# A feed-forward, attention, feed-forward layer: the setup rewritten, and each feed-forward's first tokens prepared in the block ahead of it

## What is computed

```python
def _L0_ffn_ref(x, ...):
    x = _layernorm(x, norm_g, norm_b)
    se = _layernorm(slot_embeds, slot_g, slot_b) * scale
    logits = jnp.einsum('bnd,esd->bnes', x, se)
    dispatch = jax.nn.softmax(logits, axis=1)
    combine = jax.nn.softmax(logits.reshape(x.shape[0], x.shape[1], -1), axis=-1)
    slots = jnp.einsum('bnd,bnes->besd', x, dispatch)
    gate = jax.nn.gelu(jnp.einsum('besd,edf->besf', slots, Wg) + bg[None, :, None, :], approximate=False)
    up = jnp.einsum('besd,edf->besf', slots, Wu) + bu[None, :, None, :]
    eout = jnp.einsum('besf,efo->beso', gate * up, Wd) + bd[None, :, None, :]
    return jnp.einsum('bns,bso->bno', combine, eout.reshape(eout.shape[0], -1, eout.shape[-1]))
x = x + 0.5 * _L0_ffn_ref(_layernorm(x, axis=-1), ...)
x = x + _L0_attn_ref(_layernorm(x, axis=-1), ...)
x = x + 0.5 * _L0_ffn_ref(_layernorm(x, axis=-1), ...)
```

## Time and profile before

| | us |
|---|---|
| median of three runs | 1928.64 |
| profiled execution, whole | 1929.45 |
| its span, first to last instruction | 1927.7 |
| TensorE busy | 1809.2 |
| VectorE busy | 1319.5 |
| ScalarE busy | 1157.5 |
| GpSimd busy | 819.9 |

### The profile page before, as it was taken

One profiled execution on the slowest core, in us unless ns is written; L12 is line 12 of the kernel. 1 busy time (PEld: TensorE's weight loads), 2 busy tenths in 40 slices (PEclk: granted clock), 3 DMA queues, 4 the chain that ended last, 5 costly groups with the idle time before them and its releaser, 6 DMA issues. The chain is left out here.

```text
span 1927.7 us, 35483 instructions
## 1 busy us (share of the span) xinstructions
PE 1809.2 (94%) x11720; PEld 1621.2 (84%) x11720; DVE 1319.5 (68%) x2369; ACT 1157.5 (60%) x2277; POOL 819.9 (43%) x1029
## 2 busy tenths in 40 slices
PE   1999999999999999949999969999999999999998
PEld 1778888888999999949999957888888789999998
DVE  5866666664799888835555457666665558998886
ACT  1676667666565777624444428666666656567775
POOL 1332424224688755412222214234242357885553
PEclk9999999999999999979999989999999999999999
DMA  2553334323465677621121136324342516556774
GB/s 67 207 186 131 121 145 160 131 86 124 153 224 179 244 257 262 225 82 56 65 65 65 44 124 247 133 103 165 146 153 77 186 55 225 180 185 246 262 263 160
DMA packets 106668, 298.25 MB, mean 155 GB/s; under 512 B 16256, under 2 KB 56320, under 8 KB 94272
## 3 DMA queue, kind: packets, MB, share of 16 engines
q1 hardware_dynamic: 106560, 296.88, 43.2%
HBM read 187.63 MB, written 109.22 MB: 154 GB/s over the span
## 5 line engine op out<-in xcount | busy, mean ns | idle before, releaser
L115 POOL TENSOR_TENSOR pool_carrier<-minus_half 128x1 f32<-128x1 f32 x224 | 63.3, 283 | 657.0 <-PE f2bank L839 199.0
L680 ACT ACTIVATE f1r_lt<-f1bank,slot_shift 128x512 f32<-128x512 f32 x128 | 88.2, 689 | 124.0 <-PE f1bank L810 123.9
L680 ACT ACTIVATE f2r_lt<-f2bank,slot_shift 128x512 f32<-128x512 f32 x128 | 88.2, 689 | 123.4 <-PE f2bank L810 123.3
L535 DVE TENSOR_TENSOR f2r_e_lo<-f2bank,f2r_e_hi 128x512 fp32r<-128x512 f32 x128 | 82.4, 684 | 96.3 <-ACT f2r_e_hi L762 96.3
L535 DVE TENSOR_TENSOR f1r_e_lo<-f1bank,f1r_e_hi 128x512 fp32r<-128x512 f32 x128 | 82.4, 684 | 96.3 <-ACT f1r_e_hi L762 96.3
L1498 PE MATMUL f2bank<-f2c_eo,f2c_e_hi 128*128 128x258 f32 (+1 forms) x512 | 129.9, 286 | 0.5 <-DVE f2c_xout L1420 0.5
L1498 PE MATMUL f1bank<-f1c_eo,f1c_e_hi 128*128 128x258 f32 (+1 forms) x512 | 129.9, 286 | 0.5 <-DVE f1c_xout L1420 0.4
L1499 PE MATMUL f1bank<-f1c_eo,f1c_e_hi 128*128 128x256 f32 (+1 forms) x512 | 128.0, 282 | 0.0
L1499 PE MATMUL f2bank<-f2c_eo,f2c_e_hi 128*128 128x256 f32 (+1 forms) x512 | 128.0, 282 | 0.0
L1369 POOL TENSOR_TENSOR f2c_e_lo<-f2c_lt,f2c_e_hi 128x512 fp32r<-128x512 f32 x64 | 82.8, 1295 | 74.8 <-ACT f2c_e_hi L1472 74.8
L1369 POOL TENSOR_TENSOR f1c_e_lo<-f1c_lt,f1c_e_hi 128x512 fp32r<-128x512 f32 x64 | 82.8, 1295 | 74.8 <-ACT f1c_e_hi L1472 74.8
(11 more groups left out here) (321 smaller groups left out, 6624.5 us busy)
## 6 DMA issues: line engine op xcount, KB each, us to landing
logits<-f1r_lt SPq DMA_DIRECT2D x16, 2048.0 KB, 7.3
f1c_lt<-logits SPq DMA_DIRECT2D x32, 1024.0 KB, 7.2
logits<-f2r_lt SPq DMA_DIRECT2D x16, 2048.0 KB, 7.3
f2c_lt<-logits SPq DMA_DIRECT2D x32, 1024.0 KB, 7.0
f1r_xin<-in_L_attn_x SPq DMA_DIRECT2D x16, 512.0 KB, 4.6
normalized<-f1r_xin SPq DMA_DIRECT2D x16, 512.0 KB, 2.7
f1r_xback<-normalized SPq DMA_DIRECT2D x16, 512.0 KB, 8.0
f1e_raw_g<-in_L_ffn_Wg SPq DMA_DIRECT2D x16, 512.0 KB, 4.0
```

The lines of the kernel that those rows point to most:

```text
L115: pool.tensor_tensor(c["pool_carrier"][:, col:col + 1], c["minus_half"][:, 0:1], c["minus_half"][:, 0:1], ALU.add)
L535: dve.tensor_tensor(e_lo[t % 2][:, h * BANK:(h + 1) * BANK], ps_t[h][:, :], rd(e_hi[t % 2][:, h * BANK:(h + 1) * BANK]), ALU.subtract).the ...
L680: act.activation(lt[:, g, sc, :], ps_l[sc % 2][:, :], ACT.Identity, bias=c["slot_shift"][:, sc:sc + 1]).then_inc(logit_out, 1)
```

## The change

It has three parts.

1. `setup_stage`. The slot embeddings are loaded in four DMAs with a semaphore each; then the tokens of group 0, `scale`, four loads of `norm_g`, `slot_g`, `slot_b` and `norm_b` as columns (256 single elements each), three rows, the tokens of group 1 and the biases. DVE only normalizes. PE transposes the normalized embeddings, each of four units into a bank of its own, and ACT applies gain and offset per partition (`gains`, `offsets`, which POOL makes) while it reads PSUM, then makes the high part from the result. The low parts are made by DVE (units 0, 1) and POOL (2, 3). The shift is made from products on POOL and sums on DVE.
2. `first_tokens` prepares group 0 of a feed-forward in the block ahead of it: loads of groups 0 and 1, and for group 0 statistics, scale, normalization, transposes, high and low part. For f1 this is in the setup, for f2 in attention's last turns. The route no longer does this for group 0, and raises the semaphores by hand. In group 0, four units of matmuls stand ahead of the transposes of group 1, where it was one. `token_places` gives both blocks the same places in SBUF; attention's raw weights are freed after its weights block.
3. Attention's last stores are not waited for at the end of its block. The route of f2 waits for them (`x_stored`), on SP, behind the store of the first normalized tokens.

```diff
+def first_tokens(al, c, tag, tk, x_in, banks):
...
+    def load(sp, i):
+        sp.dma_start(tk.xin[i][:, :, :], x_g[i]).then_inc(loaded[i], DMA)
...
+    def scale(pool):
+        pool_wait(pool, c, mv_done, GT)
+        pool.tensor_scalar(tk.var_eps[0][:, :], tk.mv[0][:, :, 1], 1.0 + EPS, EPS * EPS, ALU.mult, ALU.add).then_inc(var_done, 1)
...
+    def hi(act):
+        for k in range(KD):
+            act.wait_ge(tr_done, k + 1)
+            act.activation(tk.xT_hi[0][:, k, :], banks[k][:, :], ACT.Copy).then_inc(hi_done, 1)
+
+    def lo(dve, k):
+        dve.wait_ge(hi_done, k + 1)
+        dve.tensor_tensor(tk.xT_lo[0][:, k, :], banks[k][:, :], rd(tk.xT_hi[0][:, k, :]), ALU.subtract).then_inc(lo_done, 1)
...
+        def embeds_lo(eng, n):
+            h, k = units[n]
+            half = slice(h * BANK, (h + 1) * BANK)
+            eng.wait_ge(hi_done, n + 1)
+            return eng.tensor_tensor(c["emb_lo"][:, k, half], weights[:, k, half], rd(c["emb_hi"][:, k, half]), ALU.subtract)
...
+            slots = prm["slot_embeds"].rearrange("e s d -> (e s) d").rearrange("(t p) d -> p t d", p=P)
+            for i in range(4):
+                sp.dma_start(emb[:, i * PER:(i + 1) * PER, :], slots[:, i * PER:(i + 1) * PER, :]).then_inc(emb_loaded[i], DMA)
+            tokens.load(sp, 0)
+            sp.dma_start(scale[:, :], row(prm["scale"])).then_inc(columns_loaded, DMA)
+            for place, v in ((c["gain"][:, :], "norm_g"), (columns[:, 0, :], "slot_g"), (columns[:, 1, :], "slot_b"),
+                             (c["shift"][:, :], "norm_b")):
+                sp.dma_start(place.unsqueeze(2), prm[v].rearrange("(k p a) -> p k a", p=P, a=1),
+                             allow_slow_non_contiguous=True).then_inc(columns_loaded, DMA)
+            for place, v in ((slot_g, "slot_g"), (norm_b, "norm_b"), (slot_b, "slot_b")):
+                sp.dma_start(place[:, :], row(prm[v])).then_inc(rows_loaded, DMA)
+            tokens.load(sp, 1)
             for i, name in enumerate(("bg", "bu")):
-                sp.dma_start(bias_rows[:, i, :], prm[name].rearrange("e (c p) -> (e c) p", p=P)).then_inc(loads, DMA)
-            sp.wait_ge(loads, LOADS * DMA)
+                sp.dma_start(bias_rows[:, i, :], prm[name].rearrange("e (c p) -> (e c) p", p=P)).then_inc(bias_loaded, DMA)
...
+            pool.wait_ge(columns_loaded, 5 * DMA)
+            pool.tensor_scalar(scaled_gain[:, :], c["gain"][:, :], scale[:, 0:1], 0.0, ALU.mult, ALU.add).then_inc(gain_step, 1)
+            pool.wait_ge(gain_step, 1)
+            pool.tensor_tensor(gains[:, :], scaled_gain[:, :], columns[:, 0, :], ALU.mult).then_inc(gain_step, 1)
+            pool.tensor_tensor(offsets[:, :], scaled_gain[:, :], columns[:, 1, :], ALU.mult).then_inc(gain_step, 1)
+            tokens.scale(pool)
+
+            pool.wait_ge(rows_loaded, 3 * DMA)
+            pool.tensor_tensor(both_g[:, :], slot_g[:, :], norm_b[:, :], ALU.mult).then_inc(row_step, 1)
+            pool.tensor_tensor(both_b[:, :], slot_b[:, :], norm_b[:, :], ALU.mult).then_inc(row_step, 1)
+            for h in range(HB):
+                half = slice(h * NSC // HB, (h + 1) * NSC // HB)
+                pool.wait_ge(row_step, 1)
+                pool.wait_ge(emb_done, (h + 1) * NSC // HB)
+                pool.tensor_tensor(product[:, half, :], emb[:, half, :], both_g[:, :].unsqueeze(1).to_broadcast([P, NSC // HB, D]),
+                                   ALU.mult).then_inc(product_done, 1)
+            for n in range(KD, KD * HB):
+                embeds_lo(pool, n).then_inc(lo_by_pool, 1)
...
+            def shift_sums(h):
+                half = slice(h * NSC // HB, (h + 1) * NSC // HB)
+                dve.wait_ge(product_done, h + 1)
+                dve.tensor_reduce(shift_sum[:, half], product[:, half, :], AX_X, ALU.add).then_inc(sum_done, 1)
...
+            tokens.statistics(dve)
             dve.wait_ge(rstd_done, 1)
             dve.wait_ge(mv_done, NSC)
             for t in range(NSC):
                 dve.tensor_scalar(emb[:, t, :], emb[:, t, :], mv[:, t, 0:1], rstd[:, t:t + 1],
-                                  ALU.subtract, ALU.mult).then_inc(emb_step, 1)
-            dve.wait_ge(emb_step, NSC)
-            dve.tensor_tensor(emb[:, :, :], emb[:, :, :], slot_g[:, :].unsqueeze(1).to_broadcast([P, NSC, D]),
-                              ALU.mult).then_inc(emb_step, 1)
-            dve.wait_ge(emb_step, NSC + 1)
-            dve.tensor_tensor(emb[:, :, :], emb[:, :, :], slot_b[:, :].unsqueeze(1).to_broadcast([P, NSC, D]),
-                              ALU.add).then_inc(emb_step, 1)
-            dve.wait_ge(emb_step, NSC + 2)
-            dve.tensor_scalar(emb[:, :, :], emb[:, :, :], scale[:, 0:1], None, ALU.mult).then_inc(emb_step, 1)
-
-            dve.wait_ge(emb_step, NSC + 3)
-            dve.tensor_tensor(shifted[:, :, :], emb[:, :, :], norm_b[:, :].unsqueeze(1).to_broadcast([P, NSC, D]),
-                              ALU.mult).then_inc(emb_step, 1)
-            dve.tensor_tensor(emb[:, :, :], emb[:, :, :], norm_g[:, :].unsqueeze(1).to_broadcast([P, NSC, D]),
-                              ALU.mult).then_inc(emb_done, 1)
-            dve.wait_ge(emb_step, NSC + 4)
-            dve.tensor_reduce(c["slot_shift"][:, :], shifted[:, :, :], AX_X, ALU.add).then_inc(emb_step, 1)
-
-            for n in range(KD * HB):
-                k, h = n // HB, n % HB
-                dve.wait_ge(hi_done, n + 1)
-                dve.tensor_tensor(c["emb_lo"][:, k, h * BANK:(h + 1) * BANK], tr[n % 2][:, :],
-                                  rd(c["emb_hi"][:, k, h * BANK:(h + 1) * BANK]), ALU.subtract).then_inc(lo_done, 1)
+                                  ALU.subtract, ALU.mult).then_inc(emb_done, 1)
+            tokens.normalize(dve)
+            for n in range(KD):
+                embeds_lo(dve, n).then_inc(lo_by_dve, 1)
+            dve.wait_ge(row_step, 2)
+            dve.tensor_reduce(shift_all[:, :], both_b[:, :], AX_X, ALU.add).then_inc(sum_done, 1)
+            for h in range(HB):
+                shift_sums(h)
+            for k in range(KD):
+                tokens.lo(dve, k)
+            dve.wait_ge(sum_done, 1 + HB)
+            dve.tensor_scalar(c["slot_shift"][:, :], shift_sum[:, :], shift_all[:, 0:1], scale[:, 0:1],
+                              ALU.add, ALU.mult).then_inc(shift_done, 1)
...
+            pe.wait_ge(gain_step, 3)
+            for n, (h, k) in enumerate(units):
+                pe.wait_ge(emb_done, (h + 1) * NSC // HB)
                 for j in range(BANK // P):
...
+            for n, (h, k) in enumerate(units):
+                half = slice(h * BANK, (h + 1) * BANK)
                 act.wait_ge(tr_done, n + 1)
-                act.activation(c["emb_hi"][:, k, h * BANK:(h + 1) * BANK], tr[n % 2][:, :], ACT.Copy).then_inc(hi_done, 1)
+                act.activation(weights[:, k, half], tr[n][:, :], ACT.Identity, bias=offsets[:, k:k + 1],
+                               scale=gains[:, k:k + 1]).then_inc(weights_done, 1)
+                act.wait_ge(weights_done, n + 1)
+                act.activation(c["emb_hi"][:, k, half], weights[:, k, half], ACT.Copy).then_inc(hi_done, 1)
+            tokens.hi(act)
...
-        load_x(0, 0)
-        load_x(1, 1)
         store_xn(0, 0, 0, 0)
+        for s, value in x_stored:
+            sp.wait_ge(s, value)
         sp.wait_ge(xT_tr, KD)
         sp.wait_ge(xn_stored[0], DMA)
         load_x(2, 0)
...
-        norm_scale(0, 0)
+        for s in (xs_done, var_done, rstd_done):
+            pool.sem_inc(s, 1)
         norm_scale(1, 1)
 
...
-        token_stats(0, 0)
         token_stats(1, 1)
-        normalize(0)
         normalize(1)
-        for k in range(KD):
-            transposed_lo(0, 0, k)
...
-        for k in range(KD):
-            transposed_hi(0, 0, k, False)
+        act.sem_inc(xT_hi_done, KD)
...
                     if g == 0:
+                        evict(1, 2, 3)
                         tokens_hi()
-                        evict(1, 2, 3)
...
-        transpose_tokens(0, 0, 0, 0)
+        pe.sem_inc(xT_tr, KD)
...
+                if begin:
+                    mm(1)
+                    mm(2)
+                    mm(3)
...
+                if ahead == 1:
+                    for i, s in enumerate(stored):
+                        sp.wait_ge(s, 1 + DMA)
+                        tokens.load(sp, i)
                 if before:
                     sp.wait_ge(y_done, KD * g)
                     sp.dma_start(y_g[g - 1], xout[1 - q][:, :, :]).then_inc(stored[1 - q], DMA)
...
-            for s in stored:
-                sp.wait_ge(s, 1 + NGR // 2 * DMA)
+            tokens.all_loaded(sp)
...
             groups(pool, emit)
+            tokens.scale(pool)
...
+                if ahead == 0:
+                    tokens.statistics(dve)
                 if before:
                     gated(g - 1, 1 - q)
                     gated_lo(g - 1)
                 if ahead >= 1:
                     tokens_lo(g + 1, 1 - q)
```

(11 more changed lines are left out.)

148 lines of the change are left out of this document (87 added, 61 removed).

## The result

| | before | after |
|---|---|---|
| median of the runs, us | 1928.49 | 1897.85 (1894.73 to 1901.68) |
| profiled execution, whole | 1929.45 | 1896.06 |
| its span | 1927.7 | 1894.3 |
| first mark (transpose of the row maxima, first feed-forward) | 66.42 | 46.24 |
| last store of attention issued | 1120.92 | 1101.22 |

The ratio after to before is 0.9838, 95% interval 0.9814 to 0.9861. The forecast was 1894, range 1888 to 1900. The intervals lie clear of no change: 1.6 to 1.7% faster.

What follows compares the result with a forecast made beforehand. TensorE, busy 1809.2 of 1927.7 us, bounds the kernel, so only its waits can give much. Gains of 22.5 and 12.2 sum to 34.7, taking 1929.45 to 1894.7, less 0.8 to the median: 1894, range 1888 to 1900.

Steps and rivals of the forecast that it cites:

- Loads: Setup: slots there at about 6.3, tokens at 8.3, element-wise columns at 10.8, kept 10.0 to 15.1.
- C: Rival, chance 0.02: five small setup loads cost 8.8 us each, one after another; columns at 52.3, whole 1935.4.
- B: Rival, chance 0.22: second group takes the gain, tokens 2 late or columns at 15.1 dragging setup: 1898 to 1900.
- The turns of DVE and POOL: Setup: DVE's two-input lower parts and POOL take turns at shared ports; setup end 25.0, its ends 22.3 and 29.4.
- The block boundary: Block's end to next block's first issue 0.9; attention's block ends some 0.4 after its last store's issue, plus 0.3.
- First feed-forward: Block start to first transpose of the row maxima 18.0; that mark at 43.9, was 66.42, gain 22.5.
- B1: Start of the first feed-forward's block, its first issue; forecast 25.9 where it was 37.06.
- chain: Feed-forward starts: store tokens 0, load tokens 2, statistics, POOL's lower parts, DVE's maxima; level with PE first, last in second.
- Second feed-forward: First transpose of its row maxima at 1140.7, was 1152.95, gain 12.2; PE reaches group 1 at 1134.8 to 1136.1.
- B2: Start of the second feed-forward's block, its first issue; forecast 1122.5.
- A (free running): Rival, chance 0.17: POOL and DVE don't hinder each other; setup 2.7 earlier, marks 0.5 and 1.1 earlier: 1889.6.
- D: Rival, chance 0.03: ready tokens don't help, old loads and waits stay first; only 11.2 and 2.4 gained: 1915.

Runs made afterwards that it cites:

- again: The changed kernel run once more with no edit, as yardstick: 1895.21 us, ratio 0.9832.
- products_later: Changed kernel with POOL waiting for the tokens' normalization before its two products, nothing left out: setup block 3.03 us shorter, first mark 42.25.
- no_products: Changed kernel without POOL's two products, so another shift is computed: setup end 20.21, tokens' normalization 2.17 us in place of 6.13.
- products_split: Changed kernel with POOL's two 1024-element products cut into eight of 256: normalization 2.89 us, columns to setup end 13.2, first mark 43.34.
- setup_alone: Changed kernel with only the setup's rewriting, no tokens made ready for either feed-forward: 1917.27 us.
- store_wait: Changed kernel with the wait for attention's stores back at its block's end: last store's issue to second mark 22.00 us in place of 19.76.
- unit_order: Changed kernel with group 0 back to one unit of matmuls ahead of group 1's transposes: PE waits 2.08 us in each feed-forward.
- later_timed: Changed kernel with POOL's products behind the tokens' normalization, same edit as `products_later`, now timed: 1894.57 us, ratio 0.9824.
- shift_on_pe: Changed kernel with the slots' shift made by small products on PE, without POOL's products and DVE's sums: 1893.04 us, ratio 0.9819.

## Why the prediction was right, and where it wasn't

The whole was right in its cause and nearly in its size: the medians are 3.9 and 1.2 above the forecast's 1894, and the marks of the first profile 2.3 and 2.9 later than forecast. The setup's end and the block boundary were too early; the two feed-forwards took 0.4 and 0.2 less than forecast and made up for a small part of it, the second one by luck.

- **Loads.** Columns in use at 11.08 (9.98 to 11.08 over the runs); forecast 10.8. When they landed no run shows: in all of them POOL's first use follows its `su_rstd` without a gap, so POOL didn't wait for the columns, as the forecast had it, but for its own operation before. They were there by 9.98. The 1.7 us that the forecast's upper bound takes for 256 elements doesn't follow from its row either, since a quarter of 8.8 is 2.2. The last quarter of the slots was used at 7.77, forecast 6.3, which cost about 0.8 at the slots' normalization (11.13 for 10.3); in `again` it began at 10.21. The rivals C and B's 15.1 are out.
- **The turns of DVE and POOL.** The right mechanism, put on too few operations. I counted DVE's operations with two inputs in SBUF and let the tokens' normalization, which reads one tile, run free until 14.9. It ended at 20.01. This is the step that failed: setup end 27.33, not 25.0, inside the 22.3 to 29.4 that was given for it. With the same work in another order it is 3.0 shorter (`products_later`). `no_products`, `products_later` and `products_split` show it. The Trainium skill, "SBUF — State Buffer", section "Who interferes with whom", had it: a tensor_scalar can take the shared pair of ports too, and a reduction never does. By that rule L163 had to be counted, and the trace agrees on both (6.13 for L163; 1.20 for the sum L282 beside a product). The prediction used only the part on the lock.
- **What the runs add.** One DVE instruction waits for one POOL instruction and not for POOL's queue: 0.82 each beside 256-wide products of 0.78, 2.44 beside 1024-wide ones of 2.39.
- **The block boundary.** From the setup's last operation to the first issue 1.27, forecast 0.9; at attention's end 1.85 from the store's issue, forecast 1.3. The trace names the 0.4: at the start of both blocks SP waits 0.4 for DVE's sequencer (`SPq L442 <- DVEq L577: 0.4, 1, 0.4`), which raises seven semaphores by hand there, the one of the first store as the fourth. Without ready tokens, where the first issue is a load, it is 0.87 (`setup_alone`), and the 4.36 of `store_wait` is 3.94 plus the same 0.4.
- **First feed-forward.** 17.64 from block to mark (17.5 to 17.9 in most runs), forecast 18.0. Tokens 2's statistics at B1 + 6.7 (7.1), POOL's lower parts 1.1 longer beside the maxima (1.0), chain and PE level: PE waits 0 to 0.4 ahead of group 1 in most runs. `unit_order` bears out the wait in the old order (forecast 2.6, measured 2.08).
- **Attention's end.** Forecast 0.3, nothing to be seen: first mark to S with tokens 1053.2 to 1055.6, without 1054.4 and 1055.2. A spread of 2.4 can't show 0.3.
- **Second feed-forward.** Gain 12.18 from S to the mark (32.03 to 19.85), forecast 12.5, less 0.3 for attention's end. The forecast had the chain last and PE waiting for tokens 1's lower parts; in the profile PE is last and waits for none. The chain came as forecast (statistics at B2 + 6.9 for 7.3, lower parts done at B2 + 14.5 for 14.8). But PE needed 14.8 from its first product to group 1, not the 12.1 to 13.4 of the forecast, since it stayed at 1.2 GHz for 6.0 us, in the kernel before for 3.3. So DVE's maxima waited for ACT's evictions of PE's units:

```profile
1103.00:1109.00 6.00, 5.64 (x13) 4.46 (x14) 3.17 (x13) 0.83 (x2) 1.40 (x3) 0.50 0.58 214
```
```profile
1116.32 1.22 DVE L612 TENSOR_REDUCE f2r_gmax<-f2r_lt 128x2 f32<-128x1024 f32 x1 [1.18 <-ACT f2r_lt L773]
...
1119.06 1.23 DVE L605 TENSOR_TENSOR f2r_over_chunks<-f2r_over_chunks,f2r_lt 128x1024 f32<-128x1024 f32 x1 [0.40 <-ACT f2r_lt L773]
```

  The path that sets the mark is another one than forecast; it is 1.4 to 2.7 us longer than I had it, and ends where I had put the chain. That the number (B2 + 18.0 for 18.2) came out is luck.
- **The sum.** Forecast 22.5 + 12.2 = 34.7. Profiled: 20.2 at the first mark, 0.5 less at S, 12.2 more at the second, and 1.5 from one stretch of lower clock that only the kernel before had, which the forecast didn't have; 33.4. By medians 30.6 in the first set and 33.5 in the second. By the experiments, set against `again`, the gain at the two marks is 14.5 for the setup (37.06 to 22.57), 6.7 for the first tokens, 2.2 for the wait and 10.1 for the second tokens with their order (32.03 - 19.76 - 2.2).
- **Rivals.** A (free running) is out by `no_products` and `products_split`. B's sign was right, its cause wrong: neither columns nor tokens 2 were late. D is out by the first products, 0.3 after each block's first issue.

Still open is why the whole times of `later_timed` and `shift_on_pe` show less than their marks. The stray stretches of lower clock explain part of it in a profiled execution. From the second mark to the end it is 772.5 to 773.2 where there is none, 774.7 to 775.7 with one beyond 1190 and 776.3 with two; one at 1150 to 1160 costs 0 to 1. But I can't show that they explain medians. In `later_timed` the second feed-forward's slower outcome (18.37 for 17.90) takes another 0.5.

## What to carry to other kernels

When work is moved from DVE to POOL, count every DVE operation that then lies beside it, a `tensor_scalar` from SBUF to SBUF too, and charge each with a whole POOL instruction, not with its own length. Put DVE's short operations before POOL's long ones, or cut the long ones, which cost POOL 1.8 more here. Reductions can lie beside them, and so could DVE's lower parts of the tokens, which have one input in PSUM (0.68 beside POOL's 1.26 in `products_later`). Semaphores that are raised by hand cost those who wait for them time (0.4 at each block here); the one that the first issue needs could be raised first, which no run tried. At a point where two chains are level, making one faster may gain nothing or make the other slower.

## What the runs showed of the hardware that I had not expected

- A short DVE operation of about 0.4 us took 2.44 beside a POOL operation of 2.39, and 0.82 beside pieces of 0.78.
- The same program settles into one of two interleavings at this place (6.13 or 4.24 for L163), which moves the setup's end by 0.6 to 0.8 us.
- With PE at full clock from the first product on, the mark came 0.7 us later than with the lower clock for its first 3.9 us.
- In this kernel, PE now and then runs a few us at the lower clock far from any block boundary, at places that differ between executions (near 1155, 1165, 1195, 1485, 1495, 1510, 1605), after 10 us in which it was busy for 6.4 to 8.2. Most cost 1.5 to 3 us of the way from the second mark to the end, those near 1155 up to 1.
